# Counting edges with four buffers of one-hots, and edge statistics squared where they lie

## The reference

```python
x = x + _L0_gnn_ref(relu(layernorm(x)), edge_index)          # ten hops of propagation
x = x + _L1_gnn_ref(relu(layernorm(x)), src, dst, W, b)      # softmax-weighted sums over edges
x = x + _L2_gnn_ref(relu(layernorm(x)), edge_index, edge_attr_4, ...)
x = x + _L3_gnn_ref(relu(layernorm(x)), edge_index, W1, b1, a1, W2, b2)   # two convolutions
```

```python
def _mlp(h, W, b, gamma, beta):
    h = jax.nn.relu(h @ W + b)
    mu = jnp.mean(h, axis=0)
    var = jnp.mean(jnp.square(h - mu), axis=0)
    return gamma * (h - mu) * jax.lax.rsqrt(var + EPS) + beta
edge_feat = _mlp(edge_attr, W_edge, b_edge, g_edge, beta_edge)
```

## Time and profile before

| | |
|---|---|
| Median of 3 runs | 2952.36 us (2944.57 to 2952.72) |
| Span of the profiled execution, first to last instruction | 2910.8 us |
| Own time of the profiled execution beside its span | not given apart from the runs |
| PE busy over the span | 2011.6 us (69%) |
| DVE, ACT, POOL busy | 1396.7 us (48%), 779.5 us (27%), 1002.3 us (34%) |
| Counting: first to last batch of one-hots on PE | some 60 to 620 us |
| Batches' matmuls (L585) | 1196, busy 293.1 us, idle before them 129.1 us |
| hot_w (L559) | 300, busy 297.0 us, idle before them 176.5 us |
| hot_p (L559) | 300, busy 127.4 us |

### The profile page before, as it was taken

How to read it: one execution, slowest core, us unless ns; L and a number is a source line. 1 busy time by engine, 2 the same in 40 slices (tenths; PEclk the granted TensorE clock), 3 DMA queues, 4 the chain that set the end, 5 groups by cost and what they waited for, 6 DMA issues and landing times. The chain is left out here.

```text
span 2910.8 us, 52183 instructions
## 1 busy us (share of the span) xinstructions
PE 2011.6 (69%) x15441; PEld 1617.6 (56%) x15442; DVE 1396.7 (48%) x2559; ACT 779.5 (27%) x1318; POOL 1002.3 (34%) x1142
## 2 busy tenths in 40 slices
PE   1777777769999999487555666664666666573579
PEld 0333344449999999454344555554555555463557
DVE  7857766664444444544533443433333333344542
ACT  1686466641111111111212221221222222221110
POOL 3311211130000000000077777767666767672000
PEclk9988988879999999799756566556555555556889
DMA  4211111110000002500122222222222222223000
GB/s 139 85 49 44 45 53 60 59 60 2 2 2 2 2 2 83 218 1 4 37 54 49 49 51 48 51 49 50 46 49 49 49 49 49 48 49 72 1 2 17
DMA packets 86636, 132.96 MB, mean 46 GB/s; under 512 B 48616, under 2 KB 55656, under 8 KB 86462
## 3 DMA queue, kind: packets, MB, share of 16 engines
q1 hardware_dynamic: 59214, 88.38, 9.4%
q0 software_dynamic: 25344, 38.98, 6.7%
q10 hardware_dynamic: 1904, 3.21, 0.4%
HBM read 95.89 MB, written 34.58 MB: 45 GB/s over the span
## 5 line engine op out<-in xcount | busy, mean ns | idle before, releaser
L1341 POOL DMA_INDIRECT counts<-p_rows,rows x784 | 837.9, 1069 | 339.2 <-issue 245.5
L929 PE MATMUL ps_hop<-y,counts 128*128 128x192 f16 x6250 | 525.2, 247 | 25.4 <-DVEq L816 14.1
L929 PEld LDWEIGHTS ps_hop<-y,counts 128*128 128x128 f16 x6250 | 520.0, 98 | 30.5 <-DVEq L816 14.2
L1510 PE MATMUL ps_e_z<-e_w_q,counts 128*128 128x96 f32 x1584 | 323.5, 389 | 307.4 <-issue 201.3
L1510 PEld LDWEIGHTS ps_e_z<-e_w_q,counts 128*128 128x128 f32 x1584 | 308.7, 299 | 341.7 <-issue 229.0
L1521 PE MATMUL ps_e_seg<-counts 128*128 128x96 f32 x1584 | 325.7, 370 | 166.5 <-issue 150.6
L1521 PEld LDWEIGHTS ps_e_seg<-counts 128*128 128x128 f32 x1584 | 296.4, 277 | 217.7 <-issue 216.4
L585 PE MATMUL ps_counts<-hot_w,hot_p 128*128 x1196 | 293.1, 377 | 129.1 <-DVE hot_p L559 77.5
L559 DVE TENSOR_TENSOR hot_w<-iota_w,places_now 128x1600 f16<-128x1600 f16 x300 | 297.0, 990 | 176.5 <-PE ps_counts L585 160.2
L1468 ACT ACTIVATE counts<-ps_e_u 96x1024 f32<-96x1024 f32 x99 | 101.0, 1020 | 823.0 <-remote 563.1
L1399 DVE SCALAR_TENSOR_TENSOR seg<-ps_e_seg,part_masks,seg 128x96 f32 x196 | 52.8, 311 | 511.5 <-remote 490.2
(11 more groups left out here) (343 smaller groups left out, 2151.6 us busy)
## 6 DMA issues: line engine op xcount, KB each, us to landing
counts<-count_rows SPq DMA_DIRECT2D x30, 800.0 KB, 6.6
count_rows<-attr_split SPq DMA_DIRECT2D x25, 800.0 KB, 3.8
counts<-p_rows,rows POOLq DMA_INDIRECT x784
e_attr<-attr_parts SPq DMA_DIRECT2D x99, 72.0 KB
attr_parts<-attr_split SPq DMA_DIRECT2D x9, 784.0 KB, 15.8
attr<-attr_parts SPq DMA_DIRECT2D x50, 140.6 KB
e_dst_rows<-dst_row SPq DMA_DIRECT2D x99, 64.0 KB
e_w_q<-q_rows SPq DMA_DIRECT2D x396, 12.0 KB
```

The lines of the kernel that those rows point to most:

```text
L929: mm = pe.matmul(ps[:, r, 0:2 * D], k.counts[:, m, b, :], y[:, odd, b, :], start=b == 0, stop=b == NB - 1)
L1341: nc.gpsimd.indirect_dma_start(z[:, slot, j, :], None, k.p_rows, bass.IndirectOffsetOnAxis(rows, 0)) \
L1510: mm = pe.matmul(ps_z[:, two, j // (STEP_TILES // 2), at:at + D], u_hot[:, two, j * P:(j + 1) * P], w_q[:, fed, j // Q_TILES, :], start=Tr ...
```

## The change

Two edits, both in `count_edges`.

The first makes `hot_p` and `hot_w` a ring of four. DVE may now be four batches ahead of PE in place of two; PE reads slot i & 3.

The second removes the SBUF tensor `u`. ACT writes the rectified features back into the four PSUM banks they came from, and squares them there. PE may therefore write `ps_u` for unit n only when unit n-1 is squared: its wait goes from `u_taken` to `u_summed`. ACT's own wait for `u_summed` ahead of the rectifying is gone.

```diff
@@ -418,6 +418,7 @@
     DEGREE = BANK - 64
+    HOTS = 4
@@ -430,10 +431,9 @@
-        hot_p = sb("hot_p", [P, 2, BATCH, P], F16)
-        hot_w = sb("hot_w", [P, 2, BATCH, WIDE], F16)
+        hot_p = sb("hot_p", [P, HOTS, BATCH, P], F16)
+        hot_w = sb("hot_w", [P, HOTS, BATCH, WIDE], F16)
         attr = sb("attr", [PRODUCTS + 3, U_PARTS * U_EDGES], BF16)
-        u = sb("u", [D, U_PARTS, U_EDGES], F32)
@@ -551,7 +551,7 @@
                 for q in range(4):
-                    s = q % 2
+                    s = q % HOTS
@@ -568,7 +568,7 @@
-            pe.sem_inc(hot_used, 2)
+            pe.sem_inc(hot_used, HOTS)
@@ -583,8 +583,8 @@
-                                       hot_p[:, bass.ds(i & 1, 1), t, :].rearrange("p a s -> p (a s)"),
-                                       hot_w[:, bass.ds(i & 1, 1), t, :].rearrange("p a s -> p (a s)"),
+                                       hot_p[:, bass.ds(i & (HOTS - 1), 1), t, :].rearrange("p a s -> p (a s)"),
+                                       hot_w[:, bass.ds(i & (HOTS - 1), 1), t, :].rearrange("p a s -> p (a s)"),
@@ -608,7 +608,7 @@
                 pe.wait_ge(attr_in, n * 16 + 16)
                 if not isinstance(n, int) or n:
 
-                    pe.wait_ge(u_taken, n)
+                    pe.wait_ge(u_summed, n)
@@ -669,14 +668,12 @@
             def rectified(n):
                 act.wait_ge(u_done, n + 1)
-                if not isinstance(n, int) or n:
-                    act.wait_ge(u_summed, n)
-                nc.scalar.activation(u[:, :, :], ps_u[:, :, 0:U_EDGES], ACT.Relu,
+                nc.scalar.activation(ps_u[:, :, 0:U_EDGES], ps_u[:, :, 0:U_EDGES], ACT.Relu,
                                      accum_out=u_sums[:, 0, bass.ds(n, 1)]).then_inc(u_taken, 1)
             def squares(n):
                 act.wait_ge(u_taken, n + 1)
-                nc.scalar.activation(u[:, :, :], u[:, :, :], ACT.Square,
+                nc.scalar.activation(ps_u[:, :, 0:U_EDGES], ps_u[:, :, 0:U_EDGES], ACT.Square,
                                      accum_out=u_sums[:, 1, bass.ds(n, 1)]).then_inc(u_summed, 1)
```

## The result

The kernel before takes 2943.99 us (median of 12 runs, 2937.28 to 2952.72; the three runs known beforehand were among its slower ones), the changed one 2959.08 us (12 runs, 2953.22 to 2974.0). The ratio is 1.0059 with a 95% interval of 1.0044 to 1.0074: slower by 15 us by the medians and by some 17 by the ratio. On a second chip it is 1.0078, 1.0061 to 1.0095. The time of 2958 us that I forecast is met nearly to the microsecond, but partly by luck: the forecast added 5.3 us to a median of 2952.36, and the change costs three times as much on a base that is 8 us lower. On that base my sum would have said 2949.3 us, 10 too few.

A forecast was written before the change was run, and what follows sets the result against it. No engine full throughout the counting: DVE leads to 150 us, ACT nearly full 100 to 240, PE leads behind 350. Terms -5.5 + 12.8 - 1 - 1.0 = +5.3 us; 2910.8 + 5.3 + 41.6 gives 2958 us, range 2938 to 2972.

The forecast's parts named there:

- The ring: Blocks 0 to 4: matmuls, rectifying and squaring of units follow one another, 5.10 us a unit, 5.63 with slower matmuls.
- The ring's price, +12.8: Blocks 0 to 4: 5.2 us per unit interval, a quarter of units at low clock, adds 12.8 us.
- The clock as a rival, 13 in 100: PE's new wait puts most units at 1.2 GHz, ring 5.6 us and more: 2973 us, 13 in 100.
- Low-clock batches make PE the bound: Part of the slower-clock rival: windows of two batches become PE's own limit, +5 us for some 8 more low-clock batches.
- Four buffers, -5.5: Counting stage: four one-hot buffers save PE's real waits for batches, -5.5 us, between -1 and -21.
- Trailing ACT, -1: Ends of blocks 0 to 4: PE's wait for ACT's window copy goes, -1 us, between -3 and 0.
- Squares in PSUM, -1.0: ACT's square reads PSUM, 43 ns less on 24 intervals, -1.0 us; no change taken for writing PSUM.
- The rival of banks taken by turns: ACT reading and writing one PSUM bank must take turns, up to +88 us, 3046 us; 3 in 100.
- PE makes good what it waits: no change, 25 in 100: PE recovers the new wait within each block; wait costs +4, buffers give -5.5: 2950 us, 25 in 100.
- The hot waits are real, 17 in 100: PE's 77.5 us waiting for batches are real beyond issue, 48 go: 2915 us; part 2944 to 2945; together 17 in 100.
- 350 to 620 us keeps its length: Sign in the changed profile: the counting's stretch from 350 to 620 us keeps its length within 3 us.
- 41.6 us around the program: Profiled span 2910.8 us lies 41.6 us under the median 2952.36; that difference was taken to lie around the program.

The follow-up runs named there:

- `wait_alone`: Kernel before with only PE's wait ahead of the edge matmuls changed, to the square of the unit before; two buffers, u in SBUF: 1.0075 of before.
- `pe_kept_busy`: Changed kernel plus eight matmuls of 400 columns of zeros before PE's wait in each unit of blocks 0 to 4: 1.0039 of before.
- `psum_alone`: Kernel before with the second edit alone: two buffers, squares in PSUM, PE waits for the square: 1.0076 of before, +22 us.
- `no_ring`: Changed kernel, four buffers, but the 30 units of blocks 0 to 4 squared in SBUF and PE waiting only for the rectifying: 0.9992 of before.
- second pair of traces: Second traces, without edits, of the kernel before (2921.7 us, one run) and of the changed kernel (1.0078 of before, on another chip).
- `before_fill`: Kernel before plus four matmuls of 400 columns of zeros at the start of each block: 0.9969 of before, 2914.16 us.
- `no_ring_again`: `no_ring` run and traced again without an edit: 0.9997 of before, 2920.86 us.
- second set of four kernels: Changed kernel again, no ring with two buffers, and no ring with two fill variants, on another chip: 1.0078, 1.0006, 0.9971, 0.9977 of before (2749.69 us).

## Why the prediction was right, and where its sum was wrong

The direction of the sum and the mechanism were right, its size was not: +5.3 us forecast, +17 to +22 measured by the ratios of four comparisons (1.0059 to 1.0078). Slower by over 0.3% had 30 in 100, and it is what came; no change had 57.

- **The ring.** Right in its mechanism. PE's wait before L615 is for ACT's square, rectifyings start 0.04 us behind PE's last matmul in all 30 units, and the shortest ring is 5.08 us where I said 5.10. The longest is not the 5.6 that I gave as the upper end but 5.93 to 5.96. `wait_alone` shows that this wait by itself makes the loss.
- **The ring's price, +12.8.** This is the term that was mis-sized. I took a quarter of the units at the low clock; in blocks 1 to 4 it was more than half (12 of 23). And I took 1.55 us for their matmuls. That row, at 189.39 in the earlier trace rows, was a unit in which the clock changed; one wholly at the low clock takes 1.87, as the 1.90 in the earlier trace rows had shown. Ten of the 19 intervals inside these blocks end with such a unit. With these, they are 19 x 5.08 + 10 x 0.85 = 105.0 us, and 105.5 were measured, for 98.8 forecast and 86.6 before: +18.9 in place of +12.2. Block 0 has six intervals and not the five of the earlier trace rows, whose first line leaves out a rectifying at 91.92 us; the sixth is the first one, 6.9 us before and 6.2 after, and no part of the loss.
- **The clock as a rival, 13 in 100.** It came about in good part. The granted clock fell as it said, and `pe_kept_busy` shows 10.0 of 15.4 us in blocks 2 to 4 to be its doing (7.5 by the second trace). My forecast and this rival were not two cases but one chain, a wait that lets the clock fall, and I should have taken its row into the sum. The Trainium skill, "TensorE: Matmul & The Clock Gate", section "HAM oscillation — how this bites in real kernels", warned of it for a PE that waits for DMAs between bursts. The trace agrees in kind, here for short waits on ACT: units over 1.3 us went from 6 to 13. That doesn't account for `psum_alone`, where PE was nearly busy at the low clock.
- **Low-clock batches make PE the bound.** Shown in `psum_alone`, block 1 at 50.2 us; in the changed kernel's own trace it stayed small.
- **Four buffers, -5.5.** Between -6 and +3 by `no_ring`'s two measurements, so not refuted and not shown. Right was that most of the 77.5 us of the earlier trace rows are not waits for a buffer: four slots leave 68.9. That DVE's waits in the dense windows would shrink did not come: from 60 to 150 us they are 11.8 us for 9.3. Without the ring they do shrink, from 12.3 us with two buffers to 7.4 and 7.2 with four. In all they grew from 160.2 to 188.6 us. That is the ring and not the buffers: with two buffers and the ring they are 192 us (`psum_alone`, `wait_alone`), with four and no ring 168 and 171. PE's idle time before L585 for DVE fell by 8.6, within the 5 to 10 that I named, but by only 2.6 in the second pair of traces.
- **Trailing ACT, -1.** From the last unit of blocks 1 to 4 to the first of the next, PE's starts lie 59.0 us apart in sum for 60.9 before, 1.9 less; in the second pair of traces 56.4 for 62.3.
- **Squares in PSUM, -1.0.** Right: 49 ns less on a square for the 43 I took. The rectifying, which now writes PSUM, is 11 ns shorter too. The Trainium skill, "ScalarE: Activation LUTs", section "Step-by-step: what each stage is for", says that writing PSUM is the quicker way; the trace agrees by these 11 ns. `psum_alone` and `wait_alone` differ by 0.0001, so it decides nothing. The rival of banks taken by turns is dead.
- **PE makes good what it waits: no change, 25 in 100.** Refuted: the blocks' ends give back 1.9 us of 22, or 5.9 of 23 in the second pair of traces.
- **The hot waits are real, 17 in 100.** Refuted for the large part by the two rows of waits with two and four buffers.
- **350 to 620 us keeps its length.** Missed: 366.7 for 357.2 us in blocks 5 to 24. It was a poor test, as one program gave 360.4 and 366.7. The blocks' lengths repeat, 16.0 and 18.1 us by turns, or 15.9, 16.0, 16.2 and 16.6, and fewer low-clock microseconds don't shorten the stretch (56.7 and 366.1 in `before_fill`, 93.9 and 357.2 in before). The length goes with where the low clock falls. Of the changed kernel's units these two belong to a block of 18.04 and one of 16.01 us:

```profile
504.11 1.90 PE L615 MATMUL ps_u<-attr,w_edge 39*96 39x500 bf16 x4
...
521.42 1.04 PE L615 MATMUL ps_u<-attr,w_edge 39*96 39x500 bf16 x4
```

In blocks 10 to 24 of all 14 traces, the 69 blocks whose unit ran wholly at the low clock took 17.7 to 18.2 us and the other 141 took 15.9 to 16.7; from window 2's copy to window 3's, the stretch in which the unit's matmuls lie, are 3.94 or 3.95 us in the former and 2.12 to 2.48 in the latter. The changed kernel has 8 such blocks in either trace, before 2 and 0, but `no_ring_again` has 8 too. What decides on which blocks it falls is open.
- **41.6 us around the program.** Wrong. The span is 1.7 us under the time of its own execution (2965.67 and 2964.0; 2921.7 and 2920.0). The first trace was of a faster execution than the runs shown. The error shifted nothing, since the sum returned to the median.

Four buffers with `u` kept in SBUF, the first edit alone, wasn't run. `no_ring` stands for it, in which the 20 units from block 5 on are still squared in PSUM.

## What to carry to other kernels

When a change adds a wait, write out the ring that it closes and price it at both clock levels; if the waiting engine is TensorE, the wait itself may bring the lower one, so that the dearer price belongs into the sum. Take the low clock's price from an instruction that ran at it from end to end, not from one in which it changed. And before a second buffer is doubled, follow one slot through the timeline: "waits for DVE" in front of a batch was mostly PE's own register work, and eight matmuls of zeros in each wait of the ring won 6 to 11 us where two more buffers won nothing that can be told.

## What the runs showed of the hardware

- Matmuls of zeros count as work for the clock: eight of 400 columns, 1.51 us, in each wait of a ring of 5.08 us held it at 0.98, where 0.65 was granted without them.
- Between two chips this kernel's time differs by 6% (2923 and 2750 us), all of it in the stage of messages: from its first to its last `ps_e_z` matmul 1186 to 1206 us in every trace except those of the second set of four kernels, 1016 to 1017 in these. The counting is alike on both. The gathers differ between them. Between 1500 and 2500 us, of the changed kernel on the first chip:

```profile
L1338 POOL DMA_INDIRECT counts<-p_rows,rows x656 | 698.8, 1065 | 302.4 <-issue 217.6 <-remote 77.5 <-PE ps_e_seg L1518 7.3
```

and on the other:

```profile
L1338 POOL DMA_INDIRECT counts<-p_rows,rows x773 | 755.1, 977 | 235.6 <-issue 235.6
```

There 773 of them fit into the same time, each 977 ns for 1065. Which of it is cause and which is effect no run tells; it is why kernels were compared on one chip alone.
